# Attention block and quantized FFN on eight cores: the loads of three places move from GpSimd's DMA queue to ScalarE's

## What is computed

```python
def reference(x, Wq, bq, Wk, bk, Wv, bv, Wo, bo, wq_gate, s_gate, wq_up, s_up, wq_down, s_down):
    xn = _layernorm(x, axis=-1)
    return x + attn(xn) + ffn(xn)

def attn(x):       # 16 heads of 128, 4 K/V heads, rope, causal
    q = (x @ Wq + bq).reshape(b, t, 16, 128)
    k = (x @ Wk + bk).reshape(b, t, 4, 128)
    v = (x @ Wv + bv).reshape(b, t, 4, 128)
    q, k = _rope(q, k, t)
    scores = einsum('bhtd,bhTd->bhtT', q, k) / sqrt(128)
    return softmax(scores + causal_bias) @ v @ Wo + bo

def _qlinear(x, wq, scale):
    return einsum('bsd,hd->bsh', x, (wq.astype(float32) - 128.0) * scale[:, None])

def ffn(x):        # 5632 hidden
    return _qlinear(silu(_qlinear(x, wq_gate, s_gate)) * _qlinear(x, wq_up, s_up), wq_down, s_down)
```

## Time and profile before

| | us |
|---|---|
| median of the 2 runs shown | 8323.57 (8187.82 and 8459.32) |
| profiled execution | 8119.87 |
| its span on the slowest core (core 7) | 8118.3 |
| spans of the eight cores | 8071.0 to 8118.3 |
| PE, DVE, ACT, POOL busy | 5012.8, 2297.1, 1915.0, 288.0 |

### The profile page before, as it was taken

One profiled execution on the slowest core, in us unless ns is written; L12 is line 12 of the kernel. 1 busy time (PEld: TensorE's weight loads), 2 busy tenths in 40 slices (PEclk: granted clock), 3 DMA queues, 4 the chain that ended last, 5 costly groups with the idle time before them and its releaser, 6 DMA issues.

```text
span 8118.3 us, 82450 instructions; the slowest of 8 cores (8071.0 to 8118.3 us)
## 1 busy us (share of the span) xinstructions
PE 5012.8 (62%) x29504; PEld 2507.8 (31%) x29504; DVE 2297.1 (28%) x4914; ACT 1915.0 (24%) x2851; POOL 288.0 (4%) x514
## 2 busy tenths in 40 slices
PE   2444444446878889788788544667744467775444
PEld 1121221212333367233347411334421133442111
DVE  3555445552111122111112133321113331111222
ACT  0111111110111100111110011567741157773000
POOL 0000000000000000000001000000000000000111
PEclk9666666667888899888899777788977778897777
DMA  2111111111000012100001300000020000002333
GB/s 86 62 61 55 51 52 62 61 46 52 24 26 24 25 42 64 41 25 24 26 22 57 117 31 21 7 6 5 4 91 26 11 1 1 1 1 72 100 95 92
DMA packets 139500, 339.59 MB, mean 42 GB/s; under 512 B 18400, under 2 KB 57440, under 8 KB 129376
## 3 DMA queue, kind: packets, MB, share of 16 engines
q1 hardware_dynamic: 105600, 216.71, 8.4%
q0 software_dynamic: 33504, 117.60, 4.4%
HBM read 271.26 MB, written 62.98 MB: 41 GB/s over the span
## 4 chain that ended last, share of the span: by engine, by line
PE 49%; DVE 20%; ACT 12%; DMA 9%; issue 8%; POOL 1%; DVEq 1%; ACTq 0%; SPq 0%; POOLq 0%
PE P L259 43%; ACT ptb L239 9%; PE P L253 6%; DMA yf<-ff_scr 3%; DVE s1c L239 2%; DMA wqf<-wq 2%; DMA wof<-wo 1%; DMA ff_scr<-dst 1%; DVE P L239 1%; DVE wgbx L239 1%; DVE xnT L239 1%; DVE wubx L239 1%; DVE xnb L239 1%; DVE attb L239 1%; ACT fgo L239 1%
## 5 line engine op out<-in xcount | busy, mean ns | idle before, releaser
L239 ACT ACTIVATE ptb<-P,ccol 128x1024 bf16<-128x1024 f32 (+3 forms) x1664 | 1294.0, 817 | 563.2 <-PE P L253 349.2
L259 PE MATMUL P<-xnf,wgbx 128*128 128x512 bf16 x2816 | 807.5, 452 | 361.8 <-DVE wubx L239 361.8
L259 PE MATMUL P<-vh,ptb 128*128 128x129 bf16 x7424 | 662.7, 227 | 437.6 <-ACT ptb L239 423.0
L259 PEld LDWEIGHTS P<-vh,ptb 128*128 128x128 bf16 x7424 | 468.5, 100 | 963.1 <-issue 962.4
L259 PE MATMUL P<-wdbx,guT 128*128 128x257 bf16 x5344 | 666.9, 282 | 70.5 <-DVE dst L239 64.2
L239 DVE TENSOR_TENSOR P<-P,masks_s 128x128 f32<-128x128 f32 x1024 | 254.4, 294 | 1373.8 <-PE P L253 1372.1
L259 PE MATMUL P<-xnf,wubx 128*128 128x512 bf16 x2816 | 638.4, 380 | 0.0
L259 PEld LDWEIGHTS P<-wdbx,guT 128*128 128x128 bf16 x5344 | 534.0, 101 | 170.7 <-issue 91.6
L239 DVE TENSOR_TENSOR guT<-fgo,fgo 128x512 bf16<-128x512 f32 x176 | 121.8, 692 | 1579.8 <-ACT fgo L239 1579.8
L259 PE MATMUL P<-ident_bf,xnb 128*128 128x128 bf16 x768 | 119.1, 300 | 720.8 <-DVE xnb L239 685.8
L259 PEld LDWEIGHTS P<-xnf,wgbx 128*128 128x128 bf16 x2816 | 302.9, 112 | 826.2 <-issue 634.0
(11 more groups left out here) (126 smaller groups left out, 4414.1 us busy)
## 6 DMA issues: line engine op xcount, KB each, us to landing
xb<-x_full SPq DMA_DIRECT2D x64, 1024.0 KB, 5.0
wg<-wg SPq DMA_DIRECT2D x88, 256.0 KB, 2.7
wu<-wu SPq DMA_DIRECT2D x88, 256.0 KB, 3.0
wd<-wd SPq DMA_DIRECT2D x176, 128.0 KB, 2.1
ff_scr<-dst POOLq DMA_DIRECT2D x128, 128.0 KB, 2.2
xnq<-xo_scr SPq DMA_DIRECT2D x8, 2048.0 KB, 7.8
wqf<-wq SPq DMA_DIRECT2D x32, 512.0 KB, 4.9
xo<-x_own POOLq DMA_DIRECT2D x64, 256.0 KB, 4.3
```

Of the source, the lines that this page charges most:

```text
L239: getattr(e, m)(*aa, **kk).then_inc(s.h, 1))
L259: e.matmul(out=o, lhsT=l, rhs=r, start=st, stop=sp, skip_group_check=sk))
```

## The change

Every load that GpSimd issued in three places is issued by ScalarE: the loads of `qrope`, `kth` and `vh` at the start of each half of the heads, the odd `ft_scr` loads ahead of the output projection, and the `xo4` and `yf4` loads in its tile loop, together with the wait ahead of them. Semaphores, shapes, buffers and the stores are as they were.

```diff
         for H in range(2):
             barrier()
             if H == 0:
-                dma("gpsimd", qKV, qrope[:, 0:OWN], qcos_in[:, :])
-                dma("gpsimd", qKV, qrope[:, OWN:2 * OWN], qsin_in[:, :])
+                dma("scalar", qKV, qrope[:, 0:OWN], qcos_in[:, :])
+                dma("scalar", qKV, qrope[:, OWN:2 * OWN], qsin_in[:, :])
             rope_cnt = qKV.cnt
             ldxq0 = dma("sync", qXQ, xnq3[:, :, :], xo_pv[:, :, 0:512])
             for gl in range(2):
-                dma("gpsimd", qKVg, kth[:, gl * T:(gl + 1) * T],
+                dma("scalar", qKVg, kth[:, gl * T:(gl + 1) * T],
                     kt_scr[2 * H + gl][:, :])
-                dma("gpsimd", qKVg, vh[:, gl * 8256:(gl + 1) * 8256],
+                dma("scalar", qKVg, vh[:, gl * 8256:(gl + 1) * 8256],
                     v_scr[2 * H + gl][:, :])
...
             if ft % 2 == 0:
                 dma("sync", qP4a, f13[:, ft, :], ft_scr[ft][:, :])
             else:
-                dma("gpsimd", qP4b, f13[:, ft, :], ft_scr[ft][:, :])
+                dma("scalar", qP4b, f13[:, ft, :], ft_scr[ft][:, :])
...
             for tt in range(16):
-                wait("gpsimd", sV, ring_free[tt % 2])
-                dma("gpsimd", qXY[tt % 2], xo4[tt % 2][:],
+                wait("scalar", sV, ring_free[tt % 2])
+                dma("scalar", qXY[tt % 2], xo4[tt % 2][:],
                     x_own[tt * 128:(tt + 1) * 128, dc * 512:(dc + 1) * 512])
-                ldy = dma("gpsimd", qXY[tt % 2], yf4[tt % 2][:],
+                ldy = dma("scalar", qXY[tt % 2], yf4[tt % 2][:],
                           ff_scr[tt][:, dc * 512:(dc + 1) * 512])
```

## The result

The changed kernel is 3.3% faster: the ratio to the kernel before is 0.967, with a 95% interval of 0.962 to 0.973. Its profiled execution took 7883.35 us in place of 8119.87. The median of 11 runs is 8083.13 (7875.99 to 8221.01), that of 10 runs of the kernel before 8327.78. The forecast was 7900, with 7800 to 8085.

What follows compares the result with a forecast made beforehand. TensorE bounds the whole kernel, a load its last 650 us: 8119.87 - 289 (last stage) + 0 (starts, `ft_scr`) = 7831, + 68 offset = 7899, say 7900 us; range 7800 to 8085, its upper end from 7968 plus 136.

Steps and rivals of the forecast that it cites:

- P = 3.8: Last stage (output projection): us per tile after the change, between TensorE's floor of 3.45 and 4.1; gain 289 us.
- What is late next: nothing on GpSimd: Last stage: GpSimd keeps only the store, whose wake-up, issue and landing fit into two tiles, 7.6 us.
- L: Last stage: landing time of the `yf` load in the two-tile load loop; `wof` gave 3.3 median, 4.2 in the third block.
- my three values: Last stage: pace P of 3.1, 3.5 or 4.1 us from load loops of 6.1, 7.0 or 8.2 us for two tiles.
- The 4.4 worked out from first bytes: Last stage: the skill's first-byte times take 0.4 off `yf`'s 4.8, leaving L at 4.4 and P at 3.6.
- The starts and `ft_scr`: Moved loads at each heads-half start and the four ahead of the last stage: costed at 0; starts bounded -60 to +20 us.
- my signs of being wrong: `xo` issued behind the store's addition, landings over 6 us, later tiles' matmuls 0.43 each, or a start growing tens of us.
- Landings grow with the doubled traffic: Last stage rival: every landing 8.8 us, P 5.8, gain 168 us, time 8020 to 8060; chance 0.04.
- TensorE stays at the low clock: Last stage rival: P 6.5, gain 125 us, time 8063 (1.5%); chance 0.04.
- Only issue time: Last stage rival: loads take effect as before, 1.5 of 8.46 us saved per turn, 88 us, time 8100; chance 0.05.
- Slower: Rival at the two starts: ScalarE's loads delay SyncE's `xnq` and `wqf`, costing over 451 us; time over 8350; chance 0.03.
- The offset of 68: Whole kernel: the lower shown time, 8187.82, lies 68 us above the profiled run; added to 7831 to give 7899.

Runs made afterwards that it cites:

- pool_early: Kernel before, all DMAs still on GpSimd, with the loads of tile n+2 issued right behind the store of tile n; fastest run 7890.02 us (0.971).
- pool_loads_first: pool_early with the loads of tile n+2 issued ahead of the store of tile n; single run 7874.44 us (0.971 of the kernel before).
- ost4: Changed kernel with four `ost` (store) buffers in place of two; lower of two runs 7879.49 us (0.970 of the kernel before).
- scalar_late: Changed kernel, but ScalarE waits for the last addition of tile tt-1 before loading tile tt; single run 8046.1 us.

## Why the prediction was right, and where its numbers were off

**The mechanism and the place: right.** The store ahead of the loads in one in-order list made two buffers useless; pool_early and pool_loads_first show it with the order alone.

**The pace, P = 3.8: too low.** It was 4.66 on core 0, the slowest now, 4.19 on core 7, from which the 8.63 of before was read, and 4.46 over the cores. With 8.8 + 15 x 4.66 = 78.7 for a block, core 0 gives 315 in place of 263 us (the traces have 79.5, 79.3, 74.0 and 78.6, sum 311.4), and that is the difference between 289 and 236. Part of it is the choice of core: on core 7 itself the blocks went from 552 to 283, a gain of 269 of the 289 forecast, but the time is that of the slowest core, and that was another one afterwards. Two terms failed.

The first is the step "What is late next: nothing on GpSimd". I set wake-up and issue of the store with "a landing no longer than `yf`'s 4.8" against the 7.6 us of two tiles, and left out that VectorE's 2.09 belong in the same loop. With them it was 0.57 + 4.8 + 0.1 + 2.09 = 7.6 already, no slack at all. And the store, now issued behind two loads, landed in 5.9 (6.2 on core 0), not in 4.8 or less. (0.57 + 6.2 + 0.1 + 2.09) / 2 = 4.5 is near the 4.66 seen on core 0.

The second is L, which I took "nearer 4.2 than 3.3", from `wof`. It was 5.3 in the mean and 5.6 on core 0. (0.1 + 0.37 + 5.6 + 0.1 + 2.09) / 2 = 4.1 is the upper of my three values, and ost4, where the load sets the pace, had 4.17. The 4.4 worked out from first bytes was too low as well, and scalar_late, which changes the queue alone, shows no shorter landing on ScalarE's queue (4.4, before 4.3).

**The starts and `ft_scr`, 0: right**, within 2 us in the mean of the cores. The queue did hold SyncE's issue up, for 18 us, under cover of the same bytes.

**The breaks between blocks: right.** 31.2, 34.8 and 31.8 us, against 32.9, 30.6 and 31.8.

**What the profile after was to show.** `yf` fell in the chain and the loads are issued where I said. The rest did not come: TensorE's share of the chain rose only from 4.8% to 9.7%, a block took some 78 us and not 66, the stage from its first matmul to the end of the span 422 and not 370, and it moved 151 GB/s and not 170. The matmuls are not back to back in a block; on core 0 TensorE rests 26 times until VectorE's addition has freed a PSUM bank (47.9 us in all), and in this row it came back from such a rest with 5.08 us for 15 matmuls in place of 3.40:

```profile
7479.16 5.08 PE L259 MATMUL P<-wob,featT 128*128 128x512 bf16 x15 [2.51 <-DVE ost L239]
```

And one of my signs of being wrong appeared: a landing over 6 us, that of the store, in the median of five of the eight cores.

**The rivals.** "Landings grow with the doubled traffic" happened in part: by 1 to 3 us, and not to 8.8. "TensorE stays at the low clock" did not: the window's clock rose from 0.75 to 0.82. "Only issue time" is refuted by the gain itself, and scalar_late shows what it would have given, a pace of 7.12. The rule of the Trainium skill that the prediction names beside it ("DMA: Bandwidth & Descriptors", Issuing engines are not separate DMA queues) says that the DMAs of all issuing engines run on the same 16 DMA engines, and that issuing from several saves only the time of issuing. The traces agree with both halves: the landing of a transfer depends on what was issued ahead of it, on either queue, and the queue itself brought only issue time, 1.14 us of 8.26. The rest of the gain came from the order of the list. "Slower" did not happen.

**The sum.** The profiled execution was forecast at 7831 and took 7883, 52 more, and the fastest run was 7876. The offset of 68 that I added for an ordinary run hides that in 7900, so that 7900 came so close was luck: it lies 24 above the fastest run, while the measured median, 8083.13, lies at the very end of the range. That end was itself added up wrongly: 7968 + 136 is 8104, not 8086.

## What to carry to other kernels

An in-order list that writes store(n) ahead of load(n+1) turns two buffers into one. Look for it wherever one engine issues both, and first try to move the line, not the engine. When you remove one wait, write down the full loop of every buffer in the stage (wake-up, issue, landing, and the consumer's own time, over the number of buffers), the stores' too, and use landings of a busier stretch: here the next two limits lay within 0.4 us of each other, so deepening one of them (ost4) gave some 0.3 us a tile and deepening both gave 1.0.

## What the runs showed of the hardware

A store of 256 KB issued while no load of the stage was in flight landed in 2.7 to 3.4 us (the kernel before, medians of the cores). Issued behind two loads of its size, 1.1 us or less after the first of them, it took 5 to 6 in the mean of the cores, on GpSimd's queue and on ScalarE's alike (5.0 and 5.8), and 3.8 behind one. At the first half's start, with SyncE's `xnq` and ScalarE's six loads queued, SyncE's issue of one more load took 18.11 us on core 0, where the median `wqf` issue takes 0.33.
